# Expert stage of a gated two-layer block: tokens sorted into pages by their pair of experts

## The reference

```python
x = x + tanh(g_xattn[0]) * attention0(layernorm(x), ctx)
x = x + tanh(g_ffn[0])   * bitlinear_conv_ffn(layernorm(x))      # the "bitnet" stage
x = x + tanh(g_xattn[1]) * attention1(layernorm(x), ctx)         # with projections
x = x + tanh(g_ffn[1])   * experts(layernorm(x))

def experts(xf):                       # xf [8192, 256]; E = 8, I = 128, TOPK = 2
    scores = sigmoid(xf @ gate_weight.T)                  # [8192, 8]
    choice = scores + bias
    # 4 groups of 2 experts; the 2 groups with the largest sums stay, the others become 0
    topk_idx = top_k(masked choice, 2)
    w = scores at topk_idx, divided by their sum
    for e in range(8):
        combine = where(topk_idx == e, w, 0).sum(-1)      # 0 for six of the eight experts
        o = (silu(xf @ gate_proj[e].T) * (xf @ up_proj[e].T)) @ down_proj[e].T
        y = y + combine[:, None] * o
```

## Time and profile before

| | before |
|---|---|
| time, median of 3 runs | 1837.88 us (1836.23 to 1838.81) |
| span of the profiled execution, first to last instruction | 1828.1 us |
| time of the profiled execution itself | not listed beside the span |
| busy: TensorE, VectorE, ScalarE, GpSimd | 1542.6, 1544.6, 1185.9, 852.2 us |
| attention of layer 0, with the loads | until about 325 us |
| bitnet stage | until about 765 us |
| attention of layer 1 | until about 1250 us |
| expert stage | 1253 to 1828 us |
| DMA packets of the whole run | 49927, 68.40 MB |

### The profile page before, as it was taken

One profiled execution on the slowest core, in us unless ns is written; L12 is line 12 of the kernel. 1 busy time (PEld: TensorE's weight loads), 2 busy tenths in 40 slices (PEclk: granted clock), 3 DMA queues, 4 the chain that ended last, 5 costly groups with the idle time before them and its releaser, 6 DMA issues. The chain is left out here.

```text
span 1828.1 us, 45990 instructions
## 1 busy us (share of the span) xinstructions
PE 1542.6 (84%) x18010; PEld 1031.9 (56%) x18010; DVE 1544.6 (84%) x2913; ACT 1185.9 (65%) x1916; POOL 852.2 (47%) x926
## 2 busy tenths in 40 slices
PE   0799999567766667649999999995999999999998
PEld 0577777334444444436666666663565666666655
DVE  7799999568888898858999999986788888888885
ACT  1799999698878877528888888885233333333332
POOL 1456555157778777833333333331333333333332
PEclk9999999799999999969999999997999999999999
DMA  9300000000000000000000000000212213213211
GB/s 312 104 4 4 4 3 3 2 0 1 1 1 1 1 1 1 1 18 3 3 3 3 9 23 23 23 6 3 103 59 96 80 59 99 76 59 105 70 59 70
DMA packets 49927, 68.40 MB, mean 37 GB/s; under 512 B 10688, under 2 KB 41152, under 8 KB 49728
## 3 DMA queue, kind: packets, MB, share of 16 engines
q1 hardware_dynamic: 47360, 65.56, 10.9%
q10 hardware_dynamic: 2368, 0.02, 0.1%
HBM read 56.39 MB, written 8.65 MB: 36 GB/s over the span
## 5 line engine op out<-in xcount | busy, mean ns | idle before, releaser
L1593 POOL TENSOR_TENSOR e_a_parts<-e_act,e_a_parts 128x512 f16<-128x512 f32 x128 | 153.5, 1199 | 329.6 <-ACT e_a_parts L1564 329.6
L760 ACT ACTIVATE a_exp<-a_score_t 128x1024 f32<-128x1024 f32 x256 | 264.0, 1031 | 35.5 <-PE a_score_t L551 34.8
L1564 ACT ACTIVATE e_a_parts<-e_act 128x512 f16<-128x512 f32 x128 | 80.6, 630 | 304.0 <-DVE e_act L1396 272.4
L1140 POOL TENSOR_TENSOR b_hidden<-b_hidden,b_shifted 128x508 f32<-128x508 f32 x128 | 161.9, 1265 | 113.4 <-DVE b_hidden L990 113.4
L1278 PE MATMUL e_up_ps<-e_n_turned,e_up_t 128*128 128x512 f16 x768 | 187.8, 381 | 8.5 <-DVE e_act L1392 8.5
L1292 PE MATMUL e_out<-e_down_t,e_a_parts 128*128 128x256 f16 x1536 | 188.4, 273 | 0.8 <-POOL e_a_parts L1593 0.8
L1278 PE MATMUL e_gate<-e_n_turned,e_gate_t 128*128 128x512 f16 x768 | 187.9, 381 | 0.2 <-issue 0.2
L1292 PEld LDWEIGHTS e_out<-e_down_t,e_a_parts 128*128 128x128 f16 x1536 | 149.6, 98 | 39.0 <-POOL e_a_parts L1593 1.1
L1147 POOL TENSOR_TENSOR b_hidden<-b_hidden,b_scales 128x512 f32<-128x512 f32 x128 | 168.4, 1320 | 2.3 <-ACT b_scales L1122 2.3
L825 POOL TENSOR_TENSOR a_split<-ctx,a_split 128x256 f16<-128x256 f32 x64 | 43.0, 671 | 268.0 <-ACT a_split L779 268.0
L921 PE MATMUL b_hid<-b_x_turned,w1t 128*128 128x512 f16 x512 | 136.9, 392 | 26.4 <-DVE b_hidden L990 22.6
(11 more groups left out here) (202 smaller groups left out, 3862.9 us busy)
## 6 DMA issues: line engine op xcount, KB each, us to landing
ctx<-e_weights SPq DMA_DIRECT2D x64, 512.0 KB, 5.5
out<-x SPq DMA_DIRECT2D x16, 512.0 KB, 2.9
x<-in_x SPq DMA_DIRECT2D x3, 2048.0 KB, 19.0
ctx<-in_ctx SPq DMA_DIRECT2D x1, 4096.0 KB, 27.0
a_q_turned<-a_neg_max_t SPq DMA_DIRECT2D x256, 2.0 KB
ctx<-in_ctx SPq DMA_DIRECT2D x1, 3072.0 KB, 16.5
a_exp<-in_L_ffn_w SPq DMA_DIRECT2D x2, 1024.0 KB, 9.4
x<-in_x SPq DMA_DIRECT2D x1, 1536.0 KB, 16.4
```

What stands on the lines that cost most here:

```text
L760: nc.scalar.activation(exp32[:, u % 2, 2 * p:2 * p + 2, :], score_t[:, :].rearrange("p (g n) -> p g n", g=2), ACT.Exp, scale=DH ** -0.5 / ...
L1140: nc.gpsimd.tensor_tensor(dst, dst, shifted[:, c % 2, :].rearrange("p (t k) -> p t k", k=P)[:, :, 0:P - 1], ALU.add).then_inc(conv_ok, 1)
L1593: nc.gpsimd.tensor_tensor(a_parts[:, e % 4, 1, :], act3[:, e % 2, :], a_parts[:, e % 4, 0, :], ALU.subtract).then_inc(alo_ok, 1)
```

## The change

The expert stage is replaced. Two phases follow each other.

Routing works on pairs of tiles in float32: VectorE normalizes (`norm`), TensorE turns the pair (`turn_pair`), ScalarE copies it (`copy_pair`), TensorE makes the logits with the raw router weights (`logits_pair`). For every chunk of 16 tiles VectorE finds the two experts of each token and gives the pair a number from 1 to 28 (`classify`), computes the two weights (`weigh`), and TensorE counts, with a triangular matrix and ones over one-hot rows (`places`), how many tokens of the same pair come before each token. `new_pages` and `slots` make from that the token's slot in a list of pages of 128 tokens that hold one pair of experts each. x's tiles are now 264 elements long: behind the 256 features stand mean, reciprocal deviation, the two weights, the token's number and the two experts' offsets. GpSimd scatters these rows, 128 at a time, by 64 indirect DMAs to a DRAM tensor of 91 pages (`PAGES`, the most that 28 pairs can need). Blank rows, whose token number lies out of bounds, are written there ahead of time, during the bitnet stage.

Then, when all 64 scatters have landed, 91 pages go through a pipeline: SyncE loads a page (eight buffers, `PR`), VectorE normalizes it again (`centre`), ScalarE and GpSimd split it, TensorE turns it (four transposes) and VectorE copies it; TensorE loads the two offsets into registers and makes gate and up of the two experts alone; ScalarE's Silu, VectorE's two products with the weights, the split, four transposes and ScalarE's copy follow; six products of 256 columns give the sum, VectorE adds the input, and GpSimd scatters the page's rows to the output by an indirect DMA. A buffer is loaded again when its scatter has landed.

```diff
@@ constants
+CLASSES = EXPERTS * (EXPERTS - 1) // 2
+CT = 16
+NR = 3
+PAGES = (TILES * P + CLASSES * (P - 1)) // P
+PR = 8
+ROW = D + 8
+WEIGHT, TOKEN, FIRST = D + 2, D + 4, D + 5
@@ start_stage, block.gpsimd
+            nc.gpsimd.memset(m.blank[:], 0.0).then_inc(m.blank_made, 1)
...
@@ bitnet_stage
+            @block.sync
+            def _(sp):
+                sp.wait_ge(m.blank_made, 2)
+                sp.dma_start(m.rows.rearrange("(g p) w -> p g w", p=P), m.blank[:, None, :].broadcast_to([P, PAGES, ROW])).then_inc(m.blank_out, 16)
@@ expert_stage, block.sync
+                sp.wait_ge(scattered, 16 * TILES)
+                for g in range(PAGES):
+                    s = g % PR
+                    reach(sp, stored[s], 16 * (g // PR))
+                    sp.dma_start(page[:, s, :], rows_in[g * P:(g + 1) * P, :]).then_inc(page_in[s], 16)
@@ expert_stage, block.tensor
+                for q in range(last_pair):
+                    if q < 6:
+                        turn_expert(q // 2, q % 2)
+                    logits_pair(q)
+                    if q + 2 < last_pair:
+                        turn_pair(q + 2)
+                    if q + 2 >= pairs and (q + 2) % pairs == 4:
+                        places((q + 2) // pairs - 1)
+                places(CHUNKS - 1)
...
+                def first_products(g, chosen):
...
+                            for k in range(TOP):
+                                last = nc.tensor.matmul(both_ps[g % 2][:, k * D:(k + 1) * D], turned[:, g % 2, part, d, :],
+                                                        wt[:, wpart, d, bass.ds(chosen[k], D)], start=(n == 0 and d == 0 and k == 0),
+                                                        stop=(n == 2 and d == DC - 1), skip_group_check=True)
...
+                for s in range(PAGES + 3):
+                    if inside(s, PAGES):
+                        pe.wait_ge(page_in[s % PR], 16 * (s // PR + 1))
+                        chosen[s] = [pe.value_load(page[0:1, s % PR, FIRST + k:FIRST + k + 1].bitcast(I32), min_val=0, max_val=(EXPERTS - 1) * D)
+                                     for k in range(TOP)]
+                        turn_tokens(s)
+                    if inside(s - 1, PAGES):
+                        first_products(s - 1, chosen[s - 1])
+                    if inside(s - 3, PAGES):
+                        second_products(s - 3, chosen[s - 3])
+                    if inside(s - 2, PAGES):
+                        turn_acts(s - 2)
@@ expert_stage, block.vector
+                for j in range(CHUNKS):
...
+                    choose_groups(j)
+                    norms(0)
+                    choose_experts(j)
+                    norms(1)
+                    classify(j)
+                    norms(2, 3)
+                    weigh(j)
+                    norms(4, 5)
+                    new_pages(j)
+                    norms(6)
+                    slots(j)
+                    norms(7)
...
+                for s in range(PAGES + 4):
+                    if inside(s, PAGES):
+                        copy_tokens(s)
+                    if inside(s + 1, PAGES):
+                        centre(s + 1)
+                    if inside(s - 4, PAGES):
+                        add_input(s - 4)
+                    if inside(s - 1, PAGES):
+                        activate(s - 1)
@@ expert_stage, block.scalar
+                for s in range(PAGES + 3):
+                    if inside(s - 2, PAGES):
+                        high_acts(s - 2)
+                    if inside(s - 3, PAGES):
+                        copy_acts(s - 3)
+                    if inside(s + 1, PAGES):
+                        high(s + 1)
+                    if inside(s - 1, PAGES):
+                        make_silu(s - 1)
@@ expert_stage, block.gpsimd
+                for j in range(CHUNKS):
+                    pool.wait_ge(index_ok, j + 1)
+                    for t in range(j * CT, (j + 1) * CT):
+                        nc.gpsimd.indirect_dma_start(rows_in, bass.IndirectOffsetOnAxis(ap=index[:, t:t + 1], axis=0), m.rows_sb[:, t, :], None,
+                                                     bounds_check=PAGES * P - 1, oob_is_err=False).then_inc(scattered, 16)
...
+                def scatter(g):
+                    s = g % PR
+                    pool.wait_ge(sum_ok, g + 1)
+                    nc.gpsimd.indirect_dma_start(out_rows, bass.IndirectOffsetOnAxis(ap=page[:, s, TOKEN:TOKEN + 1].bitcast(U32), axis=0),
+                                                 page[:, s, 0:D], None, bounds_check=TILES * P - 1, oob_is_err=False).then_inc(stored[s], 16)
...
+                for s in range(PAGES + 4):
+                    if inside(s - 2, PAGES):
+                        low_acts(s - 2)
+                    if inside(s + 1, PAGES):
+                        low(s + 1)
+                    if inside(s - 4, PAGES):
+                        scatter(s - 4)
@@ build_program
+        m.rows_sb = sb("x", [P, TILES, ROW])
+        m.x = m.rows_sb[:, :, 0:D]
```

More of the change, by code:

```diff
@@ new lines, in turn_tokens @@
+                def turn_tokens(g):
+                    pe.wait_ge(low_ok, g + 1)
+                    reach(pe, in_copied, g - 1)
+                    for part in range(2):
+                        for d in range(DC):
+                            n = part * DC + d
+                            last = nc.tensor.transpose(in_ps[g % 2][:, :].bitcast(F16)[:, n * P:(n + 1) * P], parts[:, g % 2, part, d * P:(d + 1) * P],
+                                                       m.ident16[:, :])
+                    last.then_inc(in_turn, 1)
@@ L1519, in _ @@
-                write_steps(step, 2, GROUPS, lag, first=2)
+                norm(4)
+                make_low(2)
+                copy_low(1)
+                norm(5)
+                norm(6)
+                copy_low(2)
+                norm(7)
+                norm(8)
+                norm(9)
+                for part in (0, 1):
+                    source = (m.mean2, m.rstd2)[part]
+                    then(nc.vector.tensor_copy(extra[:, :, part], source[:, :]))
+                dve.wait_ge(const_ok, CONSTS)
@@ new lines, in activate @@
+                def activate(g):
+                    dve.wait_ge(silu_ok, g + 1)
+                    reach(dve, alow_ok, g - 1)
+                    for k in range(TOP):
+                        last = nc.vector.scalar_tensor_tensor(out=acts[:, g % 2, k, :], in0=both_ps[g % 2][:, k * D + P:(k + 1) * D],
+                                                              scalar=page[:, g % PR, WEIGHT + k:WEIGHT + k + 1], in1=silu[:, g % 2, k, :],
+                                                              op0=ALU.mult, op1=ALU.mult)
+                    last.then_inc(acts_ok, 1)
@@ L1570, in _, with high @@
-                write_steps(step, 2, GROUPS, lag, first=2)
+                for q in range(5, last_pair):
+                    copy_pair(q)
+                    if q % pairs == pairs - 1:
+                        probabilities(q // pairs)
+                nc.scalar.preload_act_table(ACT.Silu)
+                def high(g):
+                    act.wait_ge(centred_ok, g + 1)
+                    reach(act, in_turn, g - 1)
+                    nc.scalar.activation(parts[:, g % 2, 0, :], centred[:, g % 2, :], ACT.Copy).then_inc(high_ok, 1)
@@ L1598, in _, with const @@
-                write_steps(step, 2, GROUPS, lag, first=2)
+                def const(instruction, value):
+                    instruction.then_inc(const_ok, 1)
+                    pool.wait_ge(const_ok, value)
+                const(nc.gpsimd.memset(tri[:], 1.0), 1)
+                const(nc.gpsimd.affine_select(out=tri[:], in_=tri[:], pattern=[[1, P]], compare_op=ALU.is_gt, fill=0.0, base=0,
+                                              channel_multiplier=-1), 2)
+                const(nc.gpsimd.memset(ones[:], 1.0), 3)
```

600 lines of the change are left out of this document (293 added, 307 removed).

## The result

The changed kernel takes 1728.93 us (median of 4 runs, 1725.85 to 1730.76) against 1837.36 us before (4 runs on the same chip): a ratio of 0.9409, 95% interval 0.9397 to 0.9421, faster. The forecast was 1699 us, 30 us too low; the measured time lies inside the forecast's narrower range of 1655 to 1765 us.

A forecast was written before the change was run, and what follows sets the result against it. TensorE's columns were taken to bound the old expert stage. Routing to 1367.8 us, scatters and first load to 1390.9, and 95 steps of 3.1 end at 1689.5, 138.6 less than 1828.1: 1699 us, range 1650 to 1860, narrower 1655 to 1765.

The forecast's parts named there:

- G: GpSimd's price for issuing one indirect DMA: 1.2 us taken, between bounds of 0.39 and 3.5 us.
- (a): Page loop: TensorE's instruction stream runs ahead and hides, 2.8 us a step, 1671 us; chance 0.56 together with the forecast.
- (c): Routing and page loop: GpSimd's indirect DMA costs over 2.5 us and sets both phases, 2001 us at 3.5; chance 0.12.
- (d): Page loop: a register load holds TensorE's stream over 1.12 us; at 2.1 us each, 2022 us in all; chance 0.09.
- (b): Page loop: the ring of eight page buffers decides, 3.55 us a step, 43 us more, 1742 us; chance 0.10.
- start of the stage: Where the expert stage's first normalization starts: 1253.2 us, with 0 change from what comes before.
- start to the last chunk's indices: Routing on VectorE: 20 us before the first chunk, then 94.6; the last indices ready 1.1 us before its end.
- last 16 scatters: The last chunk's scatters to pages, exposed after routing: 16 x 1.2 = 19.2 us.
- page loop: 91 pages in 95 steps of 3.1 us, 294.5 us, then the last scatter, 1.2 + 2.9 us.
- Around the span: Median time of the runs beyond the profile's span: 9.8 us, carried unchanged.
- The step: Page loop: TensorE's instruction stream sets 3.1 us a page: 0.66 instructions, 0.25 waits, 1.4 register addresses, 0.78 register loads.
- The rest of the loop: Page loop without TensorE's instruction stream: the engines' written orders run against each other give 2.8 us a step.

The follow-up runs named there:

- e6: Changed kernel with one load for both registers of a page, unchecked, and the centring two pages ahead instead of one: 1722.1 us.
- e8: Changed kernel with one unchecked load for both registers, the centring two pages ahead and 11 page buffers instead of 8: 1681.3 us.

## Why the prediction was right, and where it was off

The direction, the phases and the size were right; G, the term with the widest bounds, came out at 1.28 us a scatter in sequence (0.97 and 0.30 to the next) against 1.2 taken. That row also agrees with the about 1 us of the Trainium skill (DMA: Bandwidth & Descriptors, "Latency and other measured facts") for GpSimd's work on a DMA. That the middle of bounds nine times apart lay so near was luck. Rivals (a), (c) and (d) didn't come about, (b) only in experiments; but the sign named for (d), TensorE idle ahead of its transposes with all inputs there, is what the changed kernel shows, at 0.55 us a step. The 30.4 us between 1699.3 and the profiled execution's 1729.7 add up by the prediction's own terms:

| term | predicted | measured | difference |
|---|---|---|---|
| start of the stage | 1253.2 | 1261.7 | +8.5 |
| start to the last chunk's indices | 113.5 | 122.5 | +9.0 |
| last 16 scatters | 19.2 | 20.9 | +1.7 |
| landing, first page load | 5.0 | 3.8 | -1.2 |
| page loop | 298.6 | 319.0 | +20.4 |
| around the span | 9.8 | 1.8 | -8.0 |

- **Around the span.** The 9.8 us were no overhead of the launch. The first profile was of an execution some 7 us shorter than the median; its stage began 8 us earlier than in the second profile. The first and the last line cancel, so by luck this error cost nothing, but the reading was wrong: the span of a profile must be held against that execution's own time.
- **Routing.** Two terms. Up to the first score it took 24.9 us, not 20, and the chunks wait three times for scores, 5.5 us in all:

```profile
DVE e_choice L1426 <- ACT e_score L1603: 5.5, 3, 2.3
```

  The prediction granted that "routing will show less" clock, but held that routing "isn't TensorE's". TensorE was granted 0.56 over the chunks, most of the time its lower level of 1.2 GHz. Eight logit products at either level:

```profile
1279.43 1.01 PE L1288 MATMUL e_bank<-router_raw,e_turned 128*128 128x8 f32 x8
...
1328.89 1.71 PE L1288 MATMUL e_bank<-router_raw,e_turned 128*128 128x8 f32 x8
```

  At that pace TensorE no longer hides behind VectorE in every chunk: from 1325 to 1338 us it is busy without a gap, and VectorE waits 1.6 us for the score behind it. VectorE's operations themselves were priced well: 4 chunks took 97.7 us with these waits, 93.5 predicted. (The prediction's "one element per 0.96 ns" is 0.96 elements per ns; its sum has it right.)
- **The step.** 3.32 us for 3.1, the term that was mis-sized: over the loop's 95 steps 21 us, which with one scatter that waits 1.66 us for "issue" about halfway and a drain that runs faster is the line's 20.4. The mechanism is the prediction's: the stream of instructions is longer than the work and sets the step. Its sum, though, came as near as it did because two errors have opposite signs. The loads take 1.30 us of it for 0.78 predicted, 0.64 each and now and then a pause, against 0.39. The rest takes 2.02 us for 2.31 (0.66 + 0.25 + 1.4): the addresses were overrated, with 12 register operations a page, 8 of 0.046 and 4 of 0.032 us, for 18 of 0.078. On TensorE's side the addresses show as products every 0.125 to 0.129 us instead of 0.109, and the loads as the 0.55 us of idle time. The Trainium skill (DMA: Bandwidth & Descriptors, "Latency and other measured facts"), cited beside rival (d), has a floor of about 600 ns for a register load: the instruction itself took 298 ns, with its arithmetic, assertion and gaps some 0.64 us, so the rule's price was nearer than the 0.39 taken.
- **The second bound.** The rest of the loop was worked out to 2.8 us; the kernels without loads stood at 3.20. The prediction's loop held the centring at its own 0.395 us. It had seen a GpSimd subtraction that "took 3.36" beside a VectorE operation and used it only as a sign that GpSimd is slow. That subtraction ended 1.99 us behind the VectorE operation's end (1260.80 and 1258.81), close to its own 2.13; with the experiments at hand it reads as a wait for that operation. With the loop at 3.2, rival (a) would have read 1709 instead of 1671 (95 x 0.4 us more); the kernel without loads took 1717.

## What to carry to other kernels

When removing the bound that a trace names brings far less than its idle time, look for an instruction elsewhere that has grown longer: a wait of one engine for another that no semaphore orders stands in a duration, not in the idle time before it. Compare durations of the same shape between kernels before believing in one bound; here three (an instruction stream with register loads at 3.3 us, VectorE and GpSimd shutting each other out at 3.2, a ring of buffers at about 3.3 once pages were taken earlier) hid behind each other. Of the combinations that were run, only the edits to all three together gave 48 us, and 58 with the centring on another engine. What an edit has removed is read from its trace: the kernel that loaded its registers once had lost the address operations too. Values for addresses are cheaper loaded several at a time and unchecked, and a stage's clock must be asked for before a half-idle engine is called hidden.

## What the runs showed of the hardware

- One register load by TensorE's sequencer from SBUF takes 0.297 us, two registers by one instruction 0.533; a bounds check adds 0.151 + 0.018 us and gaps, 0.64 us a load in the stream. The operation that makes a product's address takes 0.032 or 0.046 us.
- An indirect DMA of 128 rows of 1 KB takes GpSimd 0.97 to 1.0 us, the next one starts 0.30 later, and its data lands 2.4 us after the issue (median).
- VectorE's 0.40 us tensor_scalar with per-partition scalars, all in SBUF, and GpSimd's subtractions in SBUF exclude each other: one of them waits until the other is nearly or quite done (up to 1.95 us in a centring), and a stride in the output doesn't change it. Beside a GpSimd indirect DMA both were seen: in e6 a centring that began 0.46 us into one took 0.71 us and ended 0.17 us behind it; in e8 four that began 0.25 to 0.42 us into one took their usual 0.40.
- In every kernel with pages the 50th scatter of results comes late, its wait put to "issue" on GpSimd (1.66 us in the changed kernel, 1.57 to 2.96 over all). What it waits for stayed open.
